# Softmax weights scaled before their transposes, and the value product in four column tiles, in a two-layer graph kernel

## The reference

```
# first half, for l in 0, 1:
u = (h Wl^T h^T) or (h Wr^T h^T), by triangle of adj      # per graph 128x128
att = exp(u)*adj / (sum(exp(u)*adj) + 1e-10)
h = relu(layer_norm(att @ (h Wlin^T + b)))
x = layernorm(x + h)
# second half
q, k, v = x Wq^T, x Wk^T, x Wv^T + bv                     # 12 heads of 32
scores = q k^T / sqrt(384) + 2*adj
scores = where(any(scores != 0, axis=-1), scores, -inf)   # a row of zeros gives 0
out = nan_to_num(softmax(scores)) @ v
x = layernorm(x + out Wo^T + bo)
```

## Time and profile before

| | |
|---|---|
| median of 3 runs | 2787.65 us (2786.99 to 2789.58) |
| the profiled execution | 2786.43 us, with a span of 2784.6 us |
| mean granted clock of TensorE | 0.993 of full speed |
| TensorE matmul busy | 2733.9 us (98%), 27072 instructions |
| VectorE busy | 2374.0 us (85%), 8170 instructions |
| ScalarE busy | 1846.5 us (66%), 4363 instructions |
| GpSimd busy | 1472.7 us (53%), 1558 instructions |
| one steady pass (from the chain below) | 84.9 us |

### The profile page before, as it was taken

One profiled execution on the slowest core, in us unless ns is written; L12 is line 12 of the kernel. 1 busy time (PEld: TensorE's weight loads), 2 busy tenths in 40 slices (PEclk: granted clock), 3 DMA queues, 4 the chain that ended last, 5 costly groups with the idle time before them and its releaser, 6 DMA issues.

```text
span 2784.6 us, 74097 instructions
## 1 busy us (share of the span) xinstructions
PE 2733.9 (98%) x27072; PEld 1764.9 (63%) x27072; DVE 2374.0 (85%) x8170; ACT 1846.5 (66%) x4363; POOL 1472.7 (53%) x1558
## 2 busy tenths in 40 slices
PE   6999999999999999999999999999999999999996
PEld 3566666666666666666666666666666666666664
DVE  4888988888888889888889888898888898888986
ACT  4666676666676666776666766667666667666665
POOL 3555465455555555654455644556545556445553
PEclk9999999999999999999999999999999999999998
DMA  4011011010111010110111111101111101101000
GB/s 170 22 35 49 22 49 43 35 49 26 45 46 46 35 49 22 49 43 34 49 35 36 46 46 34 49 22 49 46 36 45 42 29 46 46 35 49 22 28 22
DMA packets 55992, 116.68 MB, mean 42 GB/s; under 512 B 4944, under 2 KB 37712, under 8 KB 55632
## 3 DMA queue, kind: packets, MB, share of 16 engines
q1 hardware_dynamic: 55632, 111.96, 11.7%
HBM read 86.77 MB, written 25.17 MB: 40 GB/s over the span
## 4 chain that ended last, share of the span: by engine, by line
PE 97%; DVE 1%; issue 1%; ACT 0%; DMA 0%; POOL 0%; SPq 0%; POOLq 0%; DVEq 0%; ACTq 0%
PE psum L1242 72%; PE psum L1252 11%; PE psum L1306 7%; PE psum L1401 4%; PE psum L1375 3%; DMA s<-weights 0%; DVE s L836 0%; DVE y L899 0%; DVE st L961 0%; DVE st L907 0%; DVE o L880 0%; DVE z L1013 0%; ACT w L582 0%; DVE pT_lo L801 0%; DVE z L1022 0%
## 5 line engine op out<-in xcount | busy, mean ns | idle before, releaser
L582 ACT ACTIVATE w<-s,nmax 128x128 f32<-128x128 f32 x1536 | 480.6, 393 | 2.4 <-DVE nmax L836 2.4
L1242 PE MATMUL psum<-hT_hi,w_hi 128*128 128x512 f16 x1152 | 438.8, 381 | 12.1 <-POOL hT_lo L377 11.9
L458 POOL TENSOR_TENSOR fold<-s 128x768 f32<-128x768 f32 x128 | 242.5, 1894 | 387.6 <-DVE nmax L836 285.7
L1242 PE MATMUL psum<-hT_lo,w_hi 128*128 128x512 f16 x1152 | 437.8, 380 | 0.0
L1242 PE MATMUL psum<-hT_hi,w_lo 128*128 128x512 f16 x1152 | 437.7, 380 | 0.0
L522 ACT ACTIVATE nT_hi<-psum 128x512 f16<-128x512 f32 x384 | 227.7, 594 | 298.9 <-PE psum L1242 296.8
L836 DVE CUSTOM_DVE_ANT_0 s<-psum,adj 128x128 f32<-128x128 f32 x1536 | 339.5, 285 | 6.1 <-DVE live L856 0.5
L385 POOL TENSOR_TENSOR hl_lo<-hl_raw,hl_hi 128x384 fp32r<-128x384 f32 x256 | 238.9, 954 | 102.6 <-ACT hl_hi L522 98.3
L803 DVE SCALAR_TENSOR_TENSOR nT_lo<-psum,nT_hi 128x512 f16<-128x512 f32 x384 | 257.7, 681 | 30.6 <-ACT nT_hi L522 30.6
L801 DVE TENSOR_TENSOR pT_lo<-psum,pT_hi 128x512 f16<-128x512 f32 x384 | 251.0, 683 | 26.1 <-ACT pT_hi L522 25.7
L522 ACT ACTIVATE pT_hi<-psum 128x512 f16<-128x512 f32 x384 | 214.6, 594 | 81.5 <-PE psum L1252 80.6
(11 more groups left out here) (135 smaller groups left out, 7934.6 us busy)
## 6 DMA issues: line engine op xcount, KB each, us to landing
xTin<-xT SPq DMA_DIRECT2D x32, 768.0 KB, 4.8
xres<-x SPq DMA_DIRECT2D x32, 768.0 KB, 4.6
out<-y SPq DMA_DIRECT2D x128, 192.0 KB, 1.9
adjm<-adjM SPq DMA_DIRECT2D x32, 384.0 KB, 5.4
adjT_sb<-adjT SPq DMA_DIRECT2D x32, 256.0 KB, 5.5
adj<-adj SPq DMA_DIRECT2D x32, 256.0 KB, 2.8
x<-weights SPq DMA_DIRECT2D x4, 576.0 KB, 4.6
s<-weights SPq DMA_DIRECT2D x3, 576.0 KB, 6.4
```

What stands on the lines that cost most here:

```text
L458: nc.gpsimd.tensor_tensor(fold[:, :, 0:n], src[:, :, 0:n], src[:, :, n:2 * n], ALU.add)\
L582: last = nc.scalar.activation(w[:, m], s[b % 2][:, m], ACT.Exp, bias=nmax[b % 2][:, m:m + 1], scale=-1.0)
L1242: last = mm(dst, a, b, start=(i == 0), stop=(i == total - 1))
```

## The change

- The softmax sum is no longer a 33rd column of `pv`. Each exponential also writes the sum of its row (`accum_out`, 12 per graph, tile `sums`).
- `w` has two buffers. `rs_of` (VectorE) takes the reciprocal of `sums` into `rcp` once the 12 exponentials of the graph are done, and then makes `rs`.
- GpSimd multiplies `w` by `rs` (`norm`, three instructions of 128x512 per graph), and `pt` waits for it (`pn_ok`).
- `pv` swaps its operands. `v` (32 columns of a head) is held, 128 columns of `pT` are streamed, and the four heads of a chunk go to four column tiles. Its result is already transposed, so `to` on TensorE and the scaling `o = psum * rs` on VectorE are gone; `hi` and `lo` of `to` read the bank of `pv`.
- `v_raw` has two of its four slots left, with a wait on `vr_lo`.
- All orders and `BANK_USES` are new. The transposes, `pv` and `po` of graphs 2 and 3 now lie in the pass after (`TAIL`), with their statistics and stores.

The code of `scores` and `u` is the same in both kernels.

```diff
@@ tiles
-        v_raw = sb("v_raw", [GROUP, FEAT])
-        v_hi, v_lo = (sb(f"v_{p}", [GROUP, HEADS, VCOL], f16) for p in ("hi", "lo"))
+        v_raw = sb("v_raw", [2, FEAT])
+        v_hi, v_lo = (sb(f"v_{p}", [GROUP, FEAT], f16) for p in ("hi", "lo"))
-        w = sb("w", [HEADS, TOK])
+        w = [sb(f"w{i}", [HEADS, TOK]) for i in range(2)]
-        o = [sb(f"o{i}", [HEADS, HEAD]) for i in range(2)]
@@ banks
-                "pt": pt_lo, "pv": o_ok, "to": to_lo, "po": y2_ok}
+                "pt": pt_lo, "pv": to_lo, "po": y2_ok}
-        TAIL = (("pv", 3), ("to", 3), ("po", 3), ("fin", 2), ("fin", 3), ("y2_power", 3), ("store", 3))
+        TAIL = (("rs", 2), ("rs", 3), ("norm", 2), ("norm", 3), ("pt", 6), ("pt", 7), ("pt", 8), ("pt", 9), ("pt", 10),
+                ("pt", 11), ("pv", 2), ("pv", 3), ("po", 2), ("po", 3), ("y2_power", 2), ("y2_power", 3), ("fin", 2),
+                ("fin", 3), ("store", 2), ("store", 3))
@@ GpSimd
+            def norm(run, b, r):
...
+                if r == 0:
+                    pool.wait_ge(rs_ok.sem, p.upto(rs_ok, b + 1))
+                part = slice(TILES * r, TILES * (r + 1))
+                nc.gpsimd.tensor_tensor(w[b % 2][:, part], w[b % 2][:, part],
+                                        rs[b % 2][:, part, None].to_broadcast([128, TILES, TOK]), ALU.mult)\
+                    .then_inc(pn_ok.sem, 1)
@@ ScalarE, exps
-                    last = nc.scalar.activation(w[:, m], s[b % 2][:, m], ACT.Exp, bias=nmax[b % 2][:, m:m + 1],
-                                                scale=-1.0)
+                    last = nc.scalar.activation(w[b % 2][:, m], s[b % 2][:, m], ACT.Exp, bias=nmax[b % 2][:, m:m + 1],
+                                                scale=-1.0, accum_out=sums[b % 2][:, m:m + 1])
@@ VectorE
             def rs_of(run, b):
-                nc.vector.reciprocal(rs[b % 2][:], src[:, :, HEAD]).then_inc(rcp_ok.sem, 1)
+                dve.wait_ge(p_ok.sem, p.upto(p_ok, (b + 1) * TILES))
+                nc.vector.reciprocal(rcp[b % 2][:], sums[b % 2][:]).then_inc(rcp_ok.sem, 1)
...
+                nc.vector.scalar_tensor_tensor(rs[b % 2][:], live[b % 2][:], 0.0, rcp[b % 2][:], ALU.is_gt, ALU.mult)\
+                    .then_inc(rs_ok.sem, 1)
-                nc.vector.tensor_tensor(o[b % 2][:].rearrange("p (c j) d -> p j c d", j=TILES), src[:, :, :, 0:HEAD],
-                                        by_tile(rs[b % 2][:])[:, :, :, None].to_broadcast([128, TILES, KB, HEAD]),
-                                        ALU.mult).then_inc(o_ok.sem, 1)
@@ TensorE
-                pe.wait_ge(p_ok.sem, p.upto(p_ok, TILES * b + r + 2))
-                turn("pt", n, [w[:, TILES * r + i] for i in range(TILES)], pt_full)
+                pe.wait_ge(pn_ok.sem, p.upto(pn_ok, n + 1))
+                turn("pt", n, [w[b % 2][:, TILES * r + i] for i in range(TILES)], pt_full)
...
-                for n in range(HEADS):
-                    h = TILES * (n % KB) + n // KB
-                    terms = split(pT_hi[b % 2][:, n], pT_lo[b % 2][:, n], v_hi[:, b, h], v_lo[:, b, h])
-                    for i, (a, m) in enumerate(terms):
-                        last = mm(dst[:, n * VCOL:(n + 1) * VCOL], a, m, start=(i == 0), stop=(i == 2))
+                for c in range(KB):
+                    for i in range(3):
+                        a, m = ((v_hi, pT_hi), (v_lo, pT_hi), (v_hi, pT_lo))[i]
+                        for j in range(TILES):
+                            d = slice(HEAD * j, HEAD * (j + 1))
+                            last = mm(dst[d, c * TOK:(c + 1) * TOK], a[:, b, c * 128 + HEAD * j:c * 128 + HEAD * (j + 1)],
+                                      m[b % 2][:, KB * j + c], start=(i == 0), stop=(i == 2))
-            def to(run, b):
...
-                turn("to", b, [of[:, k * 128:(k + 1) * 128] for k in range(KB)], to_full)
```

More of the change, by code:

```diff
@@ L319, in body @@
                         .then_inc(adjT_in.sem, 16)
-                store(p, 3)
+                for b in range(2, GROUP):
+                    store(p, b)
                 if p.l0:
@@ L325, in body @@
                         .then_inc(xres_in.sem, 16)
-                for b in range(3):
+                for b in range(2):
                     store(p, b)
@@ L598, in round_e, with pt @@
                     copy(e_hi[:, 2 * h:2 * h + 2], e[:, 2 * h:2 * h + 2]).then_inc(e_hi_ok[l].sem, 1)
-            def pt(p, b, r):
-                if not p.l1:
+            def pt(run, b, r):
+                p = run.of("pt", KB * b + r)
+                if p is None:
                     return
@@ L632, in to @@
             def to(run, b):
-                p = run.of("to", b)
+                p = run.of("pv", b)
                 if p is None:
@@ L706, in body @@
                 th(p, 2)
+                setup(p, 7)
                 exps(p, 0, 0)
+                v(p, 1)
                 exps(p, 0, 1)
@@ L763, in body @@
                 hl(p, 1, 3)
+                exps(p, 3, 2)
+                exps(p, 3, 3)
                 ctx(p, 1, 0)
@@ L839, in scores, with pt @@
                 last.then_inc(s_ok.sem, 1)
-            def pt(p, b, r):
-                if p.l1:
+            def pt(run, b, r):
+                p = run.of("pt", KB * b + r)
+                if p is not None:
                     part = slice(TILES * r, TILES * (r + 1))
@@ L852, in live_of @@
                     return
+                if b >= 2:
+                    dve.wait_ge(rs_ok.sem, p.upto(rs_ok, b - 1))
+                elif p.before.l1:
+                    dve.wait_ge(rs_ok.sem, p.before.upto(rs_ok, b + 3))
                 dve.wait_ge(fold3.sem, p.upto(fold3, b + 1))
@@ L866, in rs_of @@
+                if b >= 2:
+                    dve.wait_ge(pn_ok.sem, p.upto(pn_ok, (b - 1) * KB))
+                elif p.before.l1:
+                    dve.wait_ge(pn_ok.sem, p.before.upto(pn_ok, (b + 3) * KB))
+                dve.wait_ge(live_ok.sem, p.upto(live_ok, b + 1))
                 dve.wait_ge(rcp_ok.sem, p.upto(rcp_ok, b + 1))
[L867 to L868 removed]
@@ L1061, in v @@
                     return
+                if b >= 2:
+                    dve.wait_ge(vr_lo.sem, p.upto(vr_lo, b - 1))
+                elif p.before.l1:
+                    dve.wait_ge(vr_lo.sem, p.before.upto(vr_lo, b + 3))
                 if p.before.l1:
@@ L1150, in body @@
                 scores(p, 0, 3)
+                th(p, 0)
+                scores(p, 1, 0)
+                scores(p, 1, 1)
                 th(p, 1)
```

450 lines of the change are left out of this document (213 added, 237 removed).

## The result

The kernel after takes 2817.98 us in the median (2815.86 to 2818.46), the kernel before 2787.32 us beside it. The ratio is 1.0106 (95% interval 1.0093 to 1.0118): slower by 31 us, where 46 us faster was forecast, and outside the range.

The account below looks back on a forecast made before the run. TensorE was taken to bound the kernel, never waiting in a steady pass. Terms of -42 - 24 + 12 + 8 = -46 us took 2786.4 to 2740.4, as a median 2741.6 us; range 2716 to 2795.

Parts of the forecast that it names:

- The transposes of `o`: TensorE: dropping them saves 0.33 us a graph over 128 graphs, all on the path: -42 us.
- `pv`: TensorE: four column tiles run at the pace of `scores`, 0.71 instead of 0.90 us a graph: -24 us.
- ScalarE's accumulators: ScalarE: each exponential also writes a sum, taken at 82 ns, 3.9 us a pass, hidden: 0.
- 28 us of slack in a pass: ScalarE is busy 57.1 us of an 84.80 us pass; this slack was cited against the accumulators being dear.
- GpSimd's multiplication: GpSimd: twelve of 128x512 a pass at 1.2 us each, 14.4 us, hidden in throughput.
- The new chain at the boundary: Between two passes, exponentials to `pv`: stall of 0 to 0.75 us, taken as 0.4 a pass, +12 us.
- The lock: Start of a pass: both `scale_z` may each wait for a GpSimd multiplication's end, making `pv` wait 0.75 us.
- more room: Later in a pass: three to four `nT` or `u` groups stand before `pv` of graphs 0 and 1.
- The end: After the last `rs`: up to six multiplications, 7.2 us, with little beside them: +8 us, between 0 and 12.
- The start: The first pass: the forecast sum had no term for it.
- GpSimd and VectorE in each other's way: Rival: late `rs` delays multiplications and transposes; decides from 2.1 us a pass; 2838 us at 3.5; chance 0.16.
- I am wrong if a pass has over 2 us of waits: Sign set for failure; expected were waits under 1 us near a pass's start and passes of 83.0 to 83.5 us.

Follow-up runs that it names:

- five fixes: Four fixes, with v 2 on the bank of v 1 and its read behind those of scores(1,2) and scores(1,3): 2754.4 us, ratio 0.9885.
- Scale later: Kernel after, with VectorE's second scale_z moved behind the three pT_lo reads of graph 2: 2789.9 us, ratio 1.0005.
- tiny multiplications: Kernel after, with GpSimd's twelve multiplications a pass cut from 128x512 to 128x4x1 elements: 2772.9 us, one run.
- V first: Kernel after, with VectorE reading v 1 and v 2 before the rests of th 1 and th 2: 2799.9 us, ratio 1.0041.
- four fixes: Kernel after: second scale_z behind graph 2's pT_lo, v 1 and v 2 read earlier, th 0 on qk 5's bank, po 3 on pt 9's: 2759.0 us.
- banks only: Kernel after: second scale_z later, th 0, v 2 and po 3 on other banks, VectorE's order otherwise kept: 2848.4 us, ratio 1.0215.

## Why the prediction was wrong

- **The transposes of `o` (-42) and `pv` (-24)** were right in mechanism and in size. TensorE has 26688 instructions, and `pv` takes 0.61 to 0.62 us, or 0.71 with the step from the product ahead of it, as the earlier trace rows had it. Most of it does show once the waits are mended: with "five fixes" a pass is 84.64 - 83.25 = 1.39 us shorter than before, against (66 - 12) / 31 = 1.74 forecast. In the chain of the kernel after, and in the timeline at the end of this document:

```profile
1369.41 0.62 PE psum L1418 x36
```

- **ScalarE's accumulators (0, at 82 ns)**: 0.089 us and no cost in the kernel after, as said. The reason given, 28 us of slack in a pass, was not the right one: with the same slack the kernel before loses 22 us to them.
- **GpSimd's multiplication (1.2 us)**: 1.09, and 1891.8 us busy in all. Right.
- **The new chain at the boundary (+12, 0.4 us a pass) is the step that failed.** The prediction expected 83.0 to 83.5 us between two equal `pv`, and they are 85.51 apart. By the marks a pass went from 84.64 to 85.26; without any stall it would be 84.64 less four graphs of 0.33 + 0.19, that is 82.6, so the stalls cost 2.7 us and not 0.4. Of these 2.2 are idle time. The lock itself was foreseen rightly, both `scale_z` late by about two multiplications. But the working followed only `pv` of graph 2. It did not ask which bank the transposes ahead of it need, and so missed that `pt` 9 waits for the read of `pt` 7 a step earlier: 1.0 us plus a slower restart. "Scale later" gives back 0.91 us a pass by mending this one wait, and "tiny multiplications" 1.37 us, which is all that the multiplications cost a pass. And for the rest of the pass it said "more room", from a count of groups on TensorE. No place in the new `BANK_USES` was looked up there, and two of them hold waits of 0.84 and 0.23 us that stay when the multiplications are made tiny. "V first" gives back 0.48 us a pass; four and five fixes bring the passes to 83.37 and 83.25.
- **The end (+8)**: +7.1. The size is right, the reason only in part. Tiny multiplications take 2.4 us off the end of the kernel after and 3.4 off that of "four fixes", where up to six multiplications, 7.2 us, were the reason given. The rest was not followed, so the good agreement is partly luck.
- **The start (0)** was left out: +4.7. The first pass has no attention work to put between the steps of layer 0, and the new order of `hl`, `u` and `x1t` waits there. The kernel after has these waits of TensorE there, which the kernel before has not (us, times, longest); how much of them the 4.7 is, was not tracked down.

```profile
PE psum L1258 <- POOL hl_lo L383: 3.8, 2, 2.3
PE psum L1258 <- DVE hl_raw L837: 2.0, 2, 1.3
PE psum L1322 <- DVE nT_lo L824: 1.4, 1, 1.4
```

- **The rivals.** "GpSimd and VectorE in each other's way" decided from 2.1 us a pass, and with 2.7 us of stalls it did; its time, 2838, was too high, since it took 3.5. By "tiny multiplications" half of that was the multiplications' doing. The rest goes with order and banks (0.84 + 0.23 us of idle time above), and with the folds in the first of the two, which no rival named. Its chance of 0.16 leaned on an argument that says little: TensorE meets no wait today. The old order had been fitted to the old steps, and the change replaced the order on all four engines and the table of banks. The sentence "I am wrong if a pass has over 2 us of waits" came true to the letter.

## What to carry to other kernels

Where a change gives a new table of PSUM banks or a new order, walk through each bank's list once and ask, for each pair of neighbours, how long the reading engine has between them and what stands ahead of that read in its queue. Here 2.7 us a pass hung on that, in part made worse by what GpSimd did beside the read. An engine's slack over a pass says nothing on a place at which its result is awaited: the same 0.089 us an exponential cost 0 in one order and 0.74 us a pass in the other. And when a change with a sure gain comes out slower, move the reads before giving it up: the waits were mended one by one. Two moved reads were worth 28 and 18 us, a change of bank 13, another nothing that can be told, and the last step 3 to 5.

## What the runs showed of the hardware that was not expected

- The same wait of TensorE, 2.65 us in "banks only", was followed by a lower clock in some passes and not in others. In the one shown the granted clock was 0.50 within 1420.8 to 1423.0 and 0.81 on average to 1426.0, and behind 18 of the 30 waits it stayed at full speed. Two stretches that begin 0.5 us behind such a wait show both. What decides between them no run tells. The three waits of a pass in the kernel after, of up to 1.0 us, did not bring it: its window above has clock 1.00.

```profile
904.29:912.29 8.00, 8.00 (x76) 4.24 (x75) 5.90 (x36) 6.89 (x34) 5.18 (x6) 1.00 0.01 2
989.81:997.81 8.00, 8.00 (x67) 3.92 (x66) 4.27 (x25) 5.21 (x26) 4.79 (x5) 0.79 0.01 4
```
- A `scale_z` of VectorE (two SBUF inputs) takes 603 ns in the mean beside an idle GpSimd, and 997 ns with single ones up to 1444 ns when multiplications are added to the kernel before (the row below). By the Trainium skill (SBUF — State Buffer, Who interferes with whom) the two share a port and the later one blocks. The runs agree: with the multiplications of the kernel after made tiny it goes from 1006 ns back to 610.

```profile
L1028 DVE SCALAR_TENSOR_TENSOR z<-z,mv,lnrow x128: 586/698/1444, 81.0 to 2989.4; 128x384 f32<-128x384 f32 x128
```

- Four column tiles of 32 with 128 columns streamed run as fast as the row tiles of `scores`. From 1369.41 to 1369.74 are six rows of four, 55 ns each, and the loads of 32 columns stay hidden (timeline of the kernel after):

```profile
1369.41 0.23 PE L1418 MATMUL psum<-pT_hi,v_lo 128*32 128x128 f16 x4
...
1369.74 0.23 PE L1418 MATMUL psum<-pT_hi,v_lo 128*32 128x128 f16 x4
```
